# Cross-attention block with feed-forward: the passage from attention to the feed-forward stage, with the first accumulators loaded and biased during attention and the last two attention steps in a new order

## The reference, cut to what matters

```python
xq = layer_norm(x, qn_w, qn_b)            # x: 2 x 2048 x 512
ctx = layer_norm(context, cn_w, cn_b)     # context: 2 x 77 x 512
q = (xq @ q_w).reshape(B, N, 16, 32)
k, v = split((ctx @ kv_w).reshape(B, M, 2, 16, 32))
attn = softmax(where(mask, -FLT_MAX, q @ k^T * scale))
x = x + (attn @ v).reshape(B, N, C) @ proj_w + proj_b
h = layer_norm(x, n2_w, n2_b)
h = gelu(h @ fc1_w + fc1_b) @ fc2_w + fc2_b      # hidden width 2048
return x + h
```

## Time and profile before

| | us |
|---|---|
| median of 3 runs (lowest, highest) | 1086.98 (1083.9, 1087.06) |
| the profiled execution | 1086.47 |
| its span, first to last instruction | 1084.70 |
| PE busy in it | 1060.9 (98%) |
| DVE, ACT, POOL busy in it | 817.6, 463.0, 352.7 |

### The profile page before, as it was taken

The page is one execution under the profiler, slowest core; times in us unless marked ns, Lnnn a source line. Parts: engine busy times, 40 slices in busy tenths (PEclk is TensorE's granted clock), DMA queues, the critical chain, the costliest instruction groups (busy, mean ns, idle before and its releaser), DMA issues.

```text
span 1084.7 us, 16346 instructions
## 1 busy us (share of the span) xinstructions
PE 1060.9 (98%) x5793; PEld 867.5 (80%) x5793; DVE 817.6 (75%) x1355; ACT 463.0 (43%) x830; POOL 352.7 (33%) x257
## 2 busy tenths in 40 slices
PE   8999999999999897999999999999999999999998
PEld 6788888888888675888778888888888888888887
DVE  8888888988888767888787766677766668656655
ACT  4355355554555564455453433452343344223221
POOL 2555555655578635332604000301200120300000
PEclk9999999999999998999999999999999999999999
DMA  7011122111210067555286435344734423834322
GB/s 258 1 41 59 50 76 74 50 50 51 79 51 21 20 209 287 227 191 212 82 327 225 182 127 232 115 168 173 265 124 165 183 106 142 310 130 171 113 76 77
DMA packets 49751, 149.11 MB, mean 137 GB/s; under 512 B 8147, under 2 KB 16379, under 8 KB 41493
## 3 DMA queue, kind: packets, MB, share of 16 engines
q1 hardware_dynamic: 49101, 147.19, 37.2%
q10 hardware_dynamic: 584, 1.06, 0.3%
HBM read 108.39 MB, written 39.85 MB: 137 GB/s over the span
## 4 chain that ended last, share of the span: by engine, by line
PE 90%; DVE 4%; DMA 2%; issue 1%; POOL 1%; SPq 1%; ACT 1%; ACTq 0%; DVEq 0%
PE bank L1744 31%; PE bank L1714 27%; PE bank L1587 8%; PE bank L1544 8%; PE bank L1556 5%; PE bank L1525 4%; PE bank L1573 3%; PE bank L1723 2%; PE bank L1535 1%; DMA kvw<-in_L_xattn_kv_w 1%; PE bank L1507 1%; DMA T<-in_L_xattn_fc_w 1%; DVE ybuf L1339 1%; DVE acc L1352 0%; POOL S L633 0%
## 5 line engine op out<-in xcount | busy, mean ns | idle before, releaser
L1744 PE MATMUL bank<-w2r,gT 128*128 128x512 f32 x1536 | 361.7, 393 | 7.5 <-DVE acc L1352 7.5
L1744 PEld LDWEIGHTS bank<-w2r,gT 128*128 128x128 f32 x1536 | 288.4, 189 | 70.0 <-DVE acc L1352 9.9
L1714 PE MATMUL bank<-hop,w1r 128*128 128x512 f32 x1344 | 320.0, 396 | 0.0
L1714 PEld LDWEIGHTS bank<-hop,w1r 128*128 128x128 f32 x1344 | 251.5, 188 | 60.5 <-issue 0.7
L1352 DVE TENSOR_TENSOR acc<-bank,acc 128x512 f32<-128x512 f32 x256 | 176.7, 691 | 104.9 <-PE bank L1744 100.0
L1339 DVE TENSOR_TENSOR ybuf<-bank,ybuf 128x512 f32<-128x512 f32 x223 | 147.1, 687 | 80.4 <-PE bank L1714 75.0
L989 ACT ACTIVATE ybuf<-ybuf,cols 128x512 f32<-128x512 f32 x127 | 90.9, 716 | 163.9 <-DVE ybuf L1339 163.8
L825 ACT ACTIVATE PT<-bank 77x512 f32<-77x512 f32 x128 | 69.0, 591 | 79.6 <-PE bank L1556 78.3
L1344 DVE TENSOR_TENSOR gT<-ybuf,gT 128x512 fp32r<-128x512 f32 x127 | 96.1, 776 | 0.0
L640 POOL TENSOR_TENSOR S<-S,rsum 128x1232 f32<-128x1232 f32 x32 | 75.2, 2349 | 58.1 <-DVE rsum L1140 58.1
L633 POOL TENSOR_TENSOR S<-S,nmax 128x1232 f32<-128x1232 f32 x32 | 72.5, 2266 | 50.7 <-DVE nmax L1111 50.5
(11 more groups left out here) (112 smaller groups left out, 1436.0 us busy)
## 6 DMA issues: line engine op xcount, KB each, us to landing
w1r<-w_scratch SPq DMA_DIRECT2D x24, 1792.0 KB, 7.3
w2r<-w_scratch SPq DMA_DIRECT2D x24, 1024.0 KB, 5.2
w_scratch<-w1r SPq DMA_DIRECT2D x8, 1792.0 KB, 7.1
xr<-in_x SPq DMA_DIRECT2D x16, 512.0 KB, 3.9
x_scratch<-xr SPq DMA_DIRECT2D x16, 512.0 KB, 2.8
hring<-x_scratch SPq DMA_DIRECT2D x32, 256.0 KB, 2.8
acc<-x_scratch SPq DMA_DIRECT2D x32, 256.0 KB, 3.9
w_scratch<-w2r SPq DMA_DIRECT2D x8, 1024.0 KB, 6.6
```

Of the source, the lines that this page charges most:

```text
L1714: mm = pe.matmul(bank_[:, :], w1r[:, w1_slot(s), c, w, kk * P:(kk + 1) * P], hop[i][:, d, kk, :], start=(kk == 0 and n == 0), stop=(kk == ...
L1744: mm = pe.matmul(bY[t % 2][:, :], gT[s % 2][:, j, d, t * P:(t + 1) * P], w2r[:, s % 2, j, w, :], start=(n == 0), stop=(n == 5))
```

## The change

- Memory is laid out anew: the eight accumulators, the bias `fc2b` and places for W2 get memory that is free earlier. Accumulators 0 to 4 have a place of their own, 5 takes that of `projb`, 6 and 7 that of unit 14's `x`. T2 and T4 no longer serve for the bias and for `w2raw` 1, and one wait of `y_add` on the store of unit 15 falls away.
- Accumulators 0 to 4 are loaded by SP in steps 5 to 9 and biased by POOL in steps 6 to 10, before `less_max` 0. 5, 6 and 7 are loaded between steps 14 and 15 and biased in step 15. SP's order there: `w1raw` 1, accumulator 5, `w2raw` 0, accumulators 6 and 7, `w2raw` 1 (behind unit 15's last `prob_T`), the store of W1 of set 0, `w1raw` 2, the store of unit 15.
- POOL, step 14: `add_projb` of unit 14 stands at the head of the step, that of unit 15 behind `probs`.
- DVE and ACT, steps 14 and 15: `hop_lo` 0, `av_lo` 1, several `w1_lo`, `hop_lo`, `hop_hi` and `w1_hi` change places.
- PE, step 15: the four `mul`s of set 0 are spread between `prob_T` and `av`.
- ACT, first block: in sets 1 to 7 `w2_hi` stands behind `gelu` 3, where it stood ahead of `gelu` 0.

```diff
+    acc = [at(f"acc{t}", [P, C], F32) for t in range(BT - 3)]
+    acc.append(at(f"acc{BT - 3}", [P, C], F32, offset=projb_at))
+    acc += [at(f"acc{BT - 2 + i}", [P, C], F32, offset=xr_at + (2 * UT + i) * C * 4) for i in range(2)]
+    fc2b = at("fc2b", [P, C], F32)
...
     def w2_in(s):
-        return (T1, T4)[s] if s < 2 else w2raw
+        return T1 if s == 0 else w2raw
...
         units(0, 2, sp, step)
+        load_fc2b()
         load_w1raw(0)
         for n in range(2, NU - 1):
             if 0 <= n - LOOP[1] + 1 < BT:
                 load_h(0, n - LOOP[1] + 1)
             step(static(n), more=n + 4 < NU)
+            if 5 <= n < 5 + BT - 3:
+                load_acc(0, n - 5)
         load_h(1, 0)
         load_h(1, 1)
         load_w1raw(1)
+        p_projb.wait(sp, last_unit, UT - 1)
+        load_acc(0, BT - 3)
         load_w2raw(0)
-        v_hop.wait(sp, 0, 3)
-        p_T.wait(sp, 0, 3)
-        load_fc2b(0)
+        sp.wait_ge(d_x2st, 16 * (NU - 1))
+        load_acc(0, BT - 2)
+        load_acc(0, BT - 1)
+        load_w2raw(1)
         store_w1(0)
-        t_proj.wait(sp, last_unit, UT - 1)
-        p_projb.wait(sp, last_unit, UT - 1)
-        for t in range(BT):
-            load_acc(0, t)
+        load_w1raw(2)
         step(last_unit, more=False)
...
# POOL, step
-            late = tail in (-2, -1, 0, 1)
+            late = tail in (-2, -1, 0)
...
+            if bias is not None:
+                acc_bias(0, bias)
             if scores:
                 less_max(0)
...
-            if tail == 1:
-                add_projb(last_unit, 0)
-                add_projb(last_unit, 1)
             if scores:
                 less_max(1)
                 probs(0)
                 probs(1)
+            if tail == 1:
+                add_projb(last_unit, 0)
+                add_projb(last_unit, 1)
             if tail == 2:
+                acc_bias(0, BT - 3)
                 w1_sums(1)
+                acc_bias(0, BT - 2)
+                acc_bias(0, BT - 1)
...
# ACT, block
-                if first:
+                if first and s == 0:
                     w2_hi(s)
...
                 gelu(b, s, 1)
                 gelu(b, s, 2)
                 gelu(b, s, 3)
+                if first and s > 0:
+                    w2_hi(s)
...
# DVE, step
+            if tail == 1:
+                hop_lo(0, 0)
             if scores:
                 masked(0, 2)
                 masked(0, 3)
...
-            if tail == 2:
-                w1_lo(0, 3)
...
             if tail == 2:
+                w1_lo(0, 3)
                 hop_lo(0, 3)
...
+            if tail == 1:
+                av_lo(1)
             if scores:
                 exp_sum(0)
                 recip(0)
...
-            if back:
+            if back and tail != 1:
                 av_lo(1)
-            if tail == 1:
-                w1_lo(0, 0)
+            if tail == 2:
+                hop_lo(0, 4)
             if back:
                 av_lo(2)
-            if tail == 1:
-                hop_lo(0, 0)
-            if tail == 2:
-                y_add(0, 0, U2)
-                hop_lo(0, 4)
...
             if front:
                 q_lo(1)
+            if tail == 1:
+                w1_lo(0, 0)
+            if tail == 2:
+                y_add(0, 0, U2)
+                hop_lo(0, 5)
             if scores:
                 exp_sum(1)
                 recip(1)
...
# PE, step
-            if tail == 2:
-                mul(0, 0, M1, first=True)
-                mul(0, 0, M2, first=True)
             if back:
                 prob_T(0)
             if tail == 2:
-                mul(0, 0, M5, first=True)
+                mul(0, 0, M1, first=True)
...
+            if tail == 2:
+                mul(0, 0, M2, first=True)
             if back:
                 av(0)
                 prob_T(2)
...
+            if tail == 2:
+                mul(0, 0, M5, first=True)
             if back:
                 av(1)
-            if tail == 2:
-                mul(0, 0, M6, first=True)
-            if back:
                 prob_T(3)
                 av(2)
...
+            if tail == 2:
+                mul(0, 0, M6, first=True)
             if back:
                 av(3)
```

More of the change, by code:

```diff
@@ L192, in build_block @@
     end2 = top[0]
-    top[0] = max(end0, end2)
+    assert end0 <= ybuf_at and end2 <= 229344, (end0, ybuf_at, end2)
+    top[0] = ybuf_at
     nmax = at("nmax", [P, 2, UT, H], F32)
@@ L197, in build_block @@
     rsum = at("rsum", [P, 2, UT, H], F32)
-    assert top[0] <= 229344, (top[0], end0, end2)
     top[0] = region1
     hop = [at(f"hop{i}", [P, 2, 2, SB], F32R) for i in range(7)]
-    acc = [at(f"acc{t}", [P, C], F32) for t in range(BT - 1)]
     w2r = at("w2r", [P, 2, 2, 2, C], F32R)
[L205 to L209, removed]
+    gT1_at = top[0]
+    gT = [at("gT0", [P, 2, 2, TB], F32R, offset=PT_at), at("gT1", [P, 2, 2, TB], F32R)]
+    assert top[0] >= S1_at
     w2raw = at("w2raw", [P, 2, C], F32)
     ybuf.append(at("ybuf3", [P, SB], F32))
-    fc2b = at("fc2b", [P, C], F32)
-    assert top[0] <= projb_at
-    acc.append(at(f"acc{BT - 1}", [P, C], F32, offset=projb_at))
+    assert top[0] <= PT_at
+    w1r = at("w1r", [P, 2, 7, 2, 2 * P], F32R, offset=S0_at)
     QNW, QNB, CNW, CNB, N2W, N2B, F1B = (4 * i for i in range(7))
@@ L617, in step @@
         def step(k, back=False, scores=False, front=False, norm=False, prep=None,
-                 norm2=None, held=None, tail=None):
+                 norm2=None, held=None, tail=None, bias=None):
             def add_projb(n, t):
@@ L736, in acc_bias @@
         def acc_bias(b, t):
+            if isinstance(b, int) and b == 0 and t == 0:
+                pool.wait_ge(d_fc2b, 16)
             pool.wait_ge(d_acc[t], b * 16 + 16)
-            pool.tensor_tensor(acc[t][:, :], acc[t][:, :], bias2(b), ALU.add).then_inc(p_acc.sem, 1)
+            pool.tensor_tensor(acc[t][:, :], acc[t][:, :], fc2b[:, :], ALU.add).then_inc(p_acc.sem, 1)
         pipeline(pool, step)
@@ L750, in block @@
                     w2_lo(s)
-                if s == 0:
-                    pool.wait_ge(d_fc2b, 16 if first else 32)
+                if s == 0 and not first:
                     for t in range(BT):
@@ L875, in step @@
                 hop_hi(0, 2)
-            if tail == 2:
-                hop_hi(0, 3)
             if back:
                 prob_out(0)
-            if tail == 2:
-                w1_hi(0, 3)
-            if back:
                 prob_out(1)
@@ L917, in step @@
                 w1_hi(0, 2)
+                hop_hi(0, 3)
+                w1_hi(0, 3)
             if tail == 2:
@@ L1282, in step @@
                 recip(1)
-            if tail == 1:
-                hop_lo(0, 1)
             if tail == 2:
@@ L1287, in step @@
                 w1_lo(1, 1)
-                hop_lo(0, 5)
             if back:
                 residual(0)
+            if tail == 1:
+                hop_lo(0, 1)
             if tail == 2:
@@ L1336, in y_add @@
                 v_c.wait(dve, b, 7 * s + (U2, U3, U4)[(U3, C22, C12).index(i)])
-            if isinstance(b, int) and b == 0 and s == 1 and i == C22:
-                dve.wait_ge(d_x2st, 16 * NU)
-            dve.tensor_tensor(y_of(b, s, n), MULS[m][1][:, :], y_of(b, s, other), ALU.add).then_inc(v_c.sem, 1)
+            dve.tensor_tensor(ybuf[n][:, :], MULS[m][1][:, :], ybuf[other][:, :], ALU.add).then_inc(v_c.sem, 1)
         def g_lo(b, s, i):
```

41 lines of the change are left out of this document (15 added, 26 removed).

## The result

The changed kernel takes 1103.07 us (median of 4 runs, 1100.09 to 1104.99), the kernel before on the same chip 1085.44 (1083.53 to 1087.06). The ratio is 1.0161, with a 95% interval of 1.0129 to 1.0193: slower by 17.6 us, where 8.9 were forecast. The profiled execution took 1100.09, the shortest of the four, with a span of 1098.3: 13.6 more than before.

A forecast was written before the change was run, and what follows sets the result against it. PE was taken as the bound, busy 1060.9 of 1084.70 us. From 1086.47: -10.1 (passage, set 1) + 12.9 (sets 2 to 5) - 0.7 (set 7) gives 1088.6; + 6.8 (clock) gives 1095.4, range 1086 to 1101.

The forecast's parts named there:

- five waits for `h_T`: Block 0, sets 1 to 5: late `w2_hi` makes PE wait 3.04 us in each, bounds 2.4 and 3.6.
- The loads of accumulators 0 to 4: Attention steps 6 to 10: loading and biasing these accumulators there costs 0, up to 1 us in all.
- the passage: From attention into the first sets: set 2 starts at 426.2 instead of 436.30, 10.1 us gained, set 1's stall paid.
- The clock: Sets 1 to 5: PE's clock falls at each of five waits, 1.35 us each, 6.8 in all, bounds 0 and 9.9.
- Rival 2: Block 0's sets: the square root isn't held behind `w2_lo`, 1072.4 us; chance 0.09, shared with short waits without clock falls.
- Rival 1: Block 0's sets: the five waits come but the clock stays, 1088.6 us, bounds 1086 to 1090; chance 0.15.
- Step 14: End of attention: the projection ends at 377.15 instead of 381.83, a gain of 4.7 us (3.5 to 5.3).
- step 15: Last attention step: PE waits 1.9 us for `probs` 1 before `prob_T`, leaving 4.0 of the 4.7 us gained.
- Set 7: Block 0, set 7: PE's wait of 0.75 us goes with `w2_hi` moved, 0.7 gained.
- Sets 0 and 1: Block 0's first sets: loads of 6 to 8 us each arrive when wanted; the 6.75 us stall and its clock go.
- rival 3: Passage: loads 3 us later shrink the 10.1 gain to 7, 1098.5 us; or a clock fall in step 15, 1097; chance 0.12.

The follow-up runs named there:

- e3: Changed kernel with `h_rstd` of a set's first tile ahead of `w2_lo` on POOL, `w2_hi` still late: 1084.54 us, ratio 0.9992.
- e1: Changed kernel with `w2_hi` of sets 1 to 7 back ahead of `gelu` 0: 1083.48 us, ratio 0.9986.
- e6: Changed kernel with eleven small unused matmuls on PE before the first `h_T` of sets 1 to 5, filling its waits: 1099.82 us, ratio 1.0127.
- e8: e5 with `acc_bias` 6 and 7 put behind `w2_lo` of set 0 on POOL: 1082.32 us, ratio 0.9968.
- e4: Changed kernel with the loads of accumulators 0 to 4 issued ahead of the step's store: 1099.13 us, ratio 1.0134.
- e5: Changed kernel with both edits, e1 (`w2_hi` early) and e4 (accumulator loads earlier): 1079.42 us, ratio 0.9939.
- e10: e5 with `gT1`, `w2raw` and `ybuf3` 32 bytes higher in memory: 1085.46 us, ratio 0.9995.
- e13: e5 with `gT0` and `w1r` 416 bytes lower in memory: 1068.89 us, ratio 0.9843.
- e12: Kernel before the change with only `w1r` 32 bytes lower in memory: 1078.19 us, ratio 0.9929.
- e14: e13 with all SBUF addresses 128 bytes higher: 1069.43 us, ratio 0.9843.

## Why the prediction had the direction and not the size

The main step, five waits for `h_T` behind the late `w2_hi`, came as written, and the direction with it. The size failed in three places. The loads of accumulators 0 to 4, priced at 0, cost some 3.9 us. The new layout, which has no term at all, cost 3 to 4. And the passage was to bring set 2 10.1 us earlier and brought 5.5. The clock, priced too high, made up for part of this.

**The five waits: right.** The step "*`w2_hi` behind `gelu` 3*" gave 3.04 for each and bounds of 2.4 and 3.6. Measured: 2.50, 2.77, 2.66, 2.77 and 3.00, 13.7 in all, with `h_rstd` starting at the end of `w2_lo`. Rival 2, that the root isn't held, fell with e3: it is held, and there is little beside it (e3 is within 1.1 us of e1). Sets 2 to 5 grew by 16.4, of which 11.2 are waits and 3.0 two falls of the clock. The other 2.2 can be read too. `h_T` holds PE for 0.66 behind a wait and 0.44 without one (`472.70 0.44 PE bank L1723 x4` in the chain of the kernel before). The idle time counts only from the last matmul's modelled end, 0.39 after its start, while the next one could have started after 0.23, so 0.16 are left out. And `fc2` of sets 2 and 4, done in sets 3 and 5, takes 0.3 more: 4 x 0.22 + 4 x 0.16 + 2 x 0.3 = 2.1.

**The clock: right in kind, half the size.** Forecast were 6.8, for five falls behind the five waits. The profiled execution has two there, behind the waits of 2.77 in sets 2 and 4, and none behind 2.50, 2.66 and 3.00; a third comes behind the wait of 1.79 at set 1's start, which was not forecast. Each cost 1.5 to 1.6 (set 1's 42 matmuls take 11.42 us from start to start, for 9.80), where 1.35 was taken; e6 puts the share of those behind `h_T` at some 3. The number of falls is that of one execution, the shortest: the mean granted clock is 0.995 in it and 0.995, 0.994 and 0.992 in the other three, which suggests that some of these had more. The length of a wait doesn't decide alone: the longest had no fall, and in e1 set 1 begins with a wait of 1.89 and no fall:

```profile
405.72 10.04 PE L1708 MATMUL bank<-hop,w1r 128*128 128x512 f32 x42 [1.89 <-DVE ybuf L1333]
```

The Trainium skill ("TensorE: Matmul & The Clock Gate", section "HAM oscillation — how this bites in real kernels") lets none of these waits lower the clock; the trace disagrees three times. Rival 1, the waits without the clock, was not the case. Waits and clock together, forecast in net of set 7 as 16.2 + 6.8 - 0.7 = 22.3 (set 1's 3.3 taken out of the passage), are what e1 undoes: 19.6 by the medians.

**Step 14, step 15: right.** The projection of step 14 ends at 378.85, after an attention that came 1.5 us late: a gain of 4.5 for the 4.7 forecast. The wait before `prob_T` is 1.20, for 1.9 forecast. M7 of set 0 starts at 397.82, for 396.7 forecast; but for the 1.5 it would have been 396.3.

**Set 7: right**, 0.6 for 0.7.

**Sets 0 and 1: a wait missed.** The step said that "with 6 to 8 us each all are there when they are wanted". The loads landed about as counted: `acc_bias` 5 starts at 390.75, where 389 to 390 stood and attention came 1.5 late. But POOL had stood 6.50 us for it, with the `w1_sums` and the other biases queued behind, and the step has no term for what this work then does to DVE, which runs beside it. Two `w1_lo` take 2.66 us beside `acc_bias` and 1.03 in set 2, where POOL is idle, and `y_add` behind them comes late. PE waits 1.79 before set 1 and loses 1.6 at the fallen clock; with the late attention this made the passage's gain 5.5 instead of 10.1. It is the loss that rival 3 named, but not on its condition, loads that land 3 us later. e8 shows that the collision of `w1_lo` with the biases accounts for 1.0 of the wait; that the wait for accumulator 5 put them there is read from the trace and was not tried. The Trainium skill ("SBUF — State Buffer", section "Who interferes with whom") has DVE operations with two inputs in SBUF contend with GpSimd's reads; the trace agrees.

**Accumulators 0 to 4: wrong.** The step said that the loads "are wanted a step later. I take 0 for both, up to 1 in all". They are wanted at once. In SP's order each stands behind the step's store and the load of `x`, which waits for that store to land, so the queue is at the first of them only at 183.68 (DMA issues by time, changed kernel):

```profile
182.75 0.37 SPq L413 DMA_DIRECT2D xr<-in_x  x1
183.17 0.47 SPq L417 DMA_DIRECT2D mask_in<-in_mask_BxSxS_bk  x1
183.68 0.47 SPq L499 DMA_DIRECT2D acc<-x_scratch  x1
```

POOL is free for it at 181.74 (187.49 less the wait of 5.75), before it is even issued. The prediction weighed the bias (1.3 us) against POOL's idle time and didn't ask when the load lands. It costs 3.9 us (e4), 3.6 of them as waits of PE in the profile.

**The layout: not in the prediction at all.** The part "Memory is laid out anew" had no price. Blocks 1 to 3 take 3.3 us more in the changed kernel, and 3.7 in e5, from the start of block 1 on; twelve `fc2` at 0.31 each come to 3.7. That a slow address does this is shown by e10; a run with `gT0` alone at a fast one was not made.

What the new order is worth in itself shows in e5: set 2 starts at 425.36, 10.9 earlier than before; 13.4 were forecast for it without set 1's wait for `h_T`, 2.5 more. From there to the end e5 takes 652.7 instead of 648.4: 4.3, which I put down to the layout in all blocks. The forecast of 8.9 with the terms that were off comes to 8.9 + 3.9 (loads) + 4.3 (layout) + 2.5 (passage) - 2.7 (waits and clock) = 16.9, for 17.6 measured. That it comes so near is partly luck, since differences of medians and of single profiled executions, which lie 1 to 3 us apart, are added up in it. So the change is sound but for the place of one operation, the loads and the addresses: with all three mended, e13 is 1.6% faster than the kernel before. Part of that is no merit of the change, as `mul` had the slower pace before it too: against e12, the kernel before with `w1r` at a fast address, e13 is 9.3 us faster.

## What to carry to other kernels

When an operation is moved behind another, list what stands behind it on every engine down its chain, the smallest ones too: 0.55 us of POOL's work, queued behind a late operation, cost 18.5 us, and one edit that takes it out of that queue gave them back. For a load that is issued earlier, compare its landing with the start of its first user, in the trace, before the bias or copy that uses it is called free. After any change of layout compare the rows of code that wasn't touched: if a matmul's pace has moved there, look at the addresses of its two operands.

## What was unexpected in the hardware

The pace of dense 128x128 by 128x512 matmuls in the fp32r format (weights loaded for each) depends in these runs on the addresses in SBUF: 0.227 us where the weights' byte address in a partition and the streaming operand's are equal modulo 256, 0.2323 to 0.2334 where not, up to 2.8% more (42 matmuls in 9.52 and 9.76 to 9.80 us, 48 in 10.88 and 11.15 to 11.20). Moving both keeps the pace (e14). The tiles within an operand lie at multiples of 512 bytes here, so one difference holds for the whole operand. Why it is so was not settled; the differences that were tried are 0 and 256 modulo 512 (fast) and 32, 384 and 416 (slow), and those of operands of another width were not. What decides whether the clock falls behind a wait of 1.8 to 3 us stays open too: it fell behind 1.79 and 2.77, and didn't behind 1.89 (e1) and 3.00.
